# Complemented update gate, expert 0 inside the recurrence and 320 fixed places for each other expert

## The chip, the cores and the metric

One NeuronCore of a Trainium2 chip runs the whole program. The metric is the device time of one execution in microseconds (us), the median of a few runs. Engines are named as the profile names them: PE is TensorE (PEld its weight loads), DVE is VectorE, ACT is ScalarE, POOL is GpSimd, SP is SyncE, which here only issues DMAs.

## What is computed

Two transformer-like blocks over x (8 sequences, 256 steps, width 128; 2048 tokens). Only the recurrence and the first mixture of experts are touched:

```python
# _L0_cond2_ref: a GRU over the sequence (batch 8, 256 steps here)
r = sigmoid(xr_t + h @ W_hr)           # xr_t = x_t @ W_ir + b_ir
z = sigmoid(xz_t + h @ W_hz)
n = tanh(xn_t + r * (h @ W_hn + b_hn))
h_new = (1.0 - z) * n + z * h
# _L0_ffn_ref: top-1 routing; an expert keeps its 320 tokens of highest
# probability, the tokens dropped fall back to expert 0
final_e = where(keep, top1_idx, 0)
h = relu(tokens @ W1[e] + b1[e])       # 128 -> 512
y = h @ W2[e] + b2[e]                  # 512 -> 128, added where final_e == e
x = x + y
```

Before these stand an adaptive conditioning, a local attention and a linear attention; after them a second gated recurrence, a differential attention and a second, top-2, mixture of experts. All of it is float32; a float32 product is two passes of PE (the profile counts each).

## The kernel before

The program is a row of blocks; at the end of a block all engines wait for one another. In order: `setup`, `local_attention`, `linear_attention`, `gru_scan`, `route_top1`, `sparse_ffn`, `gate_scan`, `diff_attention`, `sparse_experts`. Every instruction order is written out by hand, with semaphores; no planner moves anything.

`gru_scan` (L782 to L956). x lies transposed, features on partitions, tokens in the order step by step, 8 tokens each. `hist` holds the states, two columns a token (the second is the state), 16 columns a step. G = 16 steps form a group; the input products of a group (`inputs`, L859) are written into PSUM ahead of time, 128 columns for each of r, z and n, and four bias rows are added by one-row products, seven products a group. In step s PE waits for the state and multiplies it by W_hr (8 columns, `pre_r`), W_hn and W_hz (`pre_n`, `pre_z`); the last two read 128 columns, the 8 states of now and 120 columns of places not yet written, whose contributions are zero (L881 to L889). Then come spare products of bf16 identities into `gspare`, three of 512 columns (`FILL`; two where an input product stands in the step). ACT: sigmoid of r (L921), sigmoid of z (L923), tanh of n (L925). DVE: a scan over 16 columns that forms xn + r * (...) (`narg`, L945), 1 - z (`keepz`, L949), z * h (`mix`, L950) and a scan that forms (1-z) * n + z * h (L953), which is the next state. Once a group the states are turned to token rows (PE L875, ACT L917) and stored in `hrow` by SP (L846). POOL clears `hist` at the start (L852), SP loads both expert weights and the biases b1 and b2 spread over the partitions (`b1B`, 2 MB). After the last step: one turn, then 16 router products (L904).

`route_top1` (L959) finds each token's expert, its probability and its rank within the expert, and `kept`. `sparse_ffn` (L1162): DVE counts the tokens of each expert, lays the experts out one after the other in blocks of 128 places (L1336 to L1369), and turns places into lists: `in_blk`, `in_lane`, a product into `f_inv` (L1380 to L1413), with the expert number of each block (L1391 to L1398). Then 23 blocks (`SLOTS`) are worked off: POOL gathers 128 rows of `hrow` (L1465), PE turns them (L1245), multiplies by W1 of the block's expert (L1254, 512 columns), DVE adds b1 (L1425), PE turns the hidden layer (L1263), ACT applies relu (L1318), PE multiplies by W2 (L1271), DVE adds b2 (L1431) and POOL scatters the rows into `frow` (L1474). POOL issues eight gathers first, then one gather and one scatter in turn. When all have landed SP reads `frow` back (L1483), PE turns it (L1294) and DVE adds it to x (L1442).

`gate_scan` (L1487) is the second recurrence, one product of 8 columns a step and 14 spare products of 128 columns.

## Time and profile before

| | us |
|---|---|
| median of 3 runs (lowest, highest) | 1709.58 (1707.33, 1715.83) |
| profiled execution | 1722.3 |
| its span, first to last instruction | 1720.3 |

| stage (from the timeline) | from, us | to, us |
|---|---|---|
| gru_scan, first step to last state | 571.6 | 1013.2 |
| its router products, to the end of the block | 1013.3 | 1021 |
| route_top1 | 1021 | 1058.7 |
| sparse_ffn, lists | 1058.7 | 1071.1 |
| sparse_ffn, 23 blocks and the way back | 1071.1 | 1155.5 |

The page gives PE 90% busy, DVE 46%, ACT 32%, POOL 8%. In a recurrence PE's busy time is mostly spare products, so the share says nothing of what bounds it; a timeline of one step does. A number after a line number is that of kernel.py.

### The profile page before, as it was taken

Reading aid. Unit: us, or ns where it says so; the run is one execution under the profiler, and the core shown is the slowest. Engines: PE = TensorE matmul, PEld = TensorE weight load, DVE = VectorE, ACT = ScalarE, POOL = GpSimd, SP = SyncE. Lnnn points to the kernel's source line nnn. Section 1 sums busy time; section 2 is a strip of 40 time slices with the busy share of each in tenths; the row PEclk is TensorE's granted clock in tenths of the full one; section 3 lists DMA queues with packets and bytes.
Section 4 is the critical chain, followed back from the end, with each engine's and each line's share of the span. In section 5 each row is a group of like instructions: output and inputs, shape, how many; then the busy total and the mean of one; then the engine's idle time right before and its main releaser. Section 6 shows DMA issues by size and latency. Waiting matters only on the chain. (4 is left out here: it accounts for less than half of the span.)

```text
span 1720.3 us, 28719 instructions
## 1 busy us (share of the span) xinstructions
PE 1541.4 (90%) x10500; PEld 1085.5 (63%) x10500; DVE 797.1 (46%) x2729; ACT 555.1 (32%) x2000; POOL 139.2 (8%) x189
## 2 busy tenths in 40 slices
PE   7999889879999899999999985879999999866995
PEld 5666556537777556566665652558888888744663
DVE  2777867655545333333333338333333333575223
ACT  2211221136554222222222220223444443533442
POOL 0000000000000000000000001630000000002662
PEclk9989998889999999999999985989999999977998
DMA  4000000000000400000000000120000000001113
GB/s 145 1 1 1 0 1 0 1 0 1 1 1 1 160 4 3 4 4 3 4 3 4 2 4 4 43 73 22 26 20 26 20 20 2 2 1 44 42 44 91
DMA packets 33892, 35.59 MB, mean 21 GB/s; under 512 B 3381, under 2 KB 27418, under 8 KB 33498
## 3 DMA queue, kind: packets, MB, share of 16 engines
q1 hardware_dynamic: 25674, 21.42, 4.1%
q0 software_dynamic: 3968, 8.13, 1.6%
q10 hardware_dynamic: 4112, 4.19, 0.8%
q8 instruction: 86, 1.41, 0.3%
q14 instruction: 52, 0.43, 0.1%
HBM read 26.53 MB, written 7.21 MB: 20 GB/s over the span
## 5 line engine op out<-in xcount | busy, mean ns | idle before, releaser
L1612 PE MATMUL spare<-identb 128*128 128x128 bf16 x3166 | 218.9, 220 | 0.0
L1612 PEld LDWEIGHTS spare<-identb 128*128 128x128 bf16 x3166 | 202.4, 103 | 4.3
L897 PE MATMUL gspare<-identb 128*128 128x512 bf16 x663 | 186.2, 381 | 0.0
L888 PEld LDWEIGHTS pre_r<-hist,gru_w 128*128 128x128 f32 x512 | 76.5, 188 | 139.0 <-DVE hist L953 138.0
L291 PE MATMUL sc<-headsel,prod 128*128 128x128 f32 x1024 | 163.3, 313 | 0.7 <-DVE prod L436 0.7
L291 PEld LDWEIGHTS sc<-headsel,prod 128*128 128x128 f32 x1024 | 141.4, 216 | 26.2 <-issue 23.9
L945 DVE TENSOR_TENSOR_SCAN narg<-rz,pre_n 128x16 f32<-128x16 f32 x256 | 48.0, 187 | 226.9 <-PE pre_n L888 226.9
L888 PE MATMUL pre_n<-hist,gru_w 128*128 128x128 f32 x512 | 121.5, 318 | 0.0
L888 PE MATMUL pre_r<-hist,gru_w 128*128 128x8 f32 x512 | 98.3, 264 | 23.9 <-DVE hist L953 2.9
L921 ACT ACTIVATE rz<-pre_r 128x8 f32<-128x8 f32 x256 | 45.7, 178 | 225.8 <-PE pre_r L888 225.8
L1663 DVE TENSOR_TENSOR_SCAN targ<-gates,pairs 128x16 f32<-128x16 f32 x256 | 49.1, 192 | 141.4 <-ACT gates L1622 141.4
L1582 PEld LDWEIGHTS s_pre<-s,wT 128*128 128x128 f32 x512 | 77.2, 190 | 40.7 <-ACT s L1625 40.0
L1582 PE MATMUL s_pre<-s,wT 128*128 128x8 f32 x512 | 98.1, 264 | 2.1 <-ACT s L1625 0.4
L888 PE MATMUL pre_z<-hist,gru_w 128*128 128x128 f32 x512 | 99.7, 275 | 0.0
L1660 DVE TENSOR_SCALAR pairs<-s,leak 128x8 f32<-128x8 f32 x256 | 59.6, 233 | 70.6 <-ACT s L1625 70.5
L1622 ACT ACTIVATE gates<-s_pre 128x8 f32<-128x8 f32 x256 | 45.6, 178 | 108.6 <-PE s_pre L1582 108.6
L1625 ACT ACTIVATE s<-targ 128x8 f32<-128x8 f32 x256 | 53.4, 209 | 83.9 <-DVE targ L1663 83.9
L485 DVE TENSOR_TENSOR term<-bc,kb 128x512 f32<-128x512 f32 x96 | 63.2, 685 | 33.2 <-PE bc L313 33.1
L888 PEld LDWEIGHTS pre_n<-hist,gru_w 128*128 128x128 f32 x512 | 78.0, 193 | 0.0
L897 PEld LDWEIGHTS gspare<-identb 128*128 128x128 bf16 x663 | 59.5, 97 | 28.8 <-issue 0.6
L888 PEld LDWEIGHTS pre_z<-hist,gru_w 128*128 128x128 f32 x512 | 77.4, 188 | 0.0
L923 ACT ACTIVATE rz<-pre_z 128x8 f32<-128x8 f32 x256 | 45.6, 178 | 97.3 <-PE pre_z L888 97.3
(413 smaller groups left out, 2531.2 us busy)
## 6 DMA issues: line engine op xcount, KB each, us to landing
w<-in_L_ffn_W SPq DMA_DIRECT2D x1, 2048.0 KB, 10.3
b1B<-in_L_ffn_b SPq DMA_DIRECT2D x1, 2048.0 KB, 19.9
raw<-in_L_ffn_wg SPq DMA_DIRECT2D x8, 256.0 KB, 3.3
raw<-in_L_ffn_wu SPq DMA_DIRECT2D x8, 256.0 KB, 2.7
raw<-in_L_ffn_wd SPq DMA_DIRECT2D x8, 256.0 KB, 2.6
wqkv<-in_L_attn_Wqkv SPq DMA_DIRECT2D x1, 1536.0 KB, 6.4
hrow<-htok SPq DMA_DIRECT2D x16, 64.0 KB, 1.5
f_back<-frow SPq DMA_DIRECT2D x4, 256.0 KB, 3.8
```

The source lines that it names most:

```text
L291: mm = nc.tensor.matmul(sc[:, :, :, :].rearrange("p i j h -> p (i j h)"), prod[u % 2][:, j, P * i:P * i + P], headsel[:, P - 2 * k:2 * P - ...
L485: nc.vector.tensor_tensor(term[s % 2][:, j, :], bc[g % 2][:, :], key(u, j, 512 * m, 512), ALU.mult).then_inc(term_done, 1)
L888: nc.tensor.matmul(out, n.gru_w[:, i, :], h, start=False, stop=True, skip_group_check=True).then_inc(ready, 1)
L897: nc.tensor.matmul(spare[:, :, :], n.identb[:, :], n.identb[:, :].unsqueeze(1).broadcast_to([P, 4, P]), start=True, stop=True)
L921: nc.scalar.activation(second(rz[s % 2][:, 0:16]), gate_slot(pre_r, s), ACT.Sigmoid).then_inc(r_done, 1)
L923: nc.scalar.activation(second(rz[s % 2][:, 16:32]), gate_slot(pre_z, s), ACT.Sigmoid).then_inc(z_done, 1)
L945: V.tensor_tensor_scan(narg[p][:, :], rz[p][:, 0:16], n_slot(s), 0.0, ALU.mult, ALU.add).then_inc(narg_done, 1)
L1582: nc.tensor.matmul(pre[s // G % 2][:, at:at + B], wT[:, 0, :], s2[:, 8 * s:8 * s + B], start=False, stop=True, skip_group_check=True).then ...
L1612: nc.tensor.matmul(spare[:, 0:P], n.identb[:, :], n.identb[:, :], start=True, stop=True)
L1625: nc.scalar.activation(s2[:, 8 * s + 8:8 * s + 16], second(targ[s % 2][:, :]), ACT.Tanh).then_inc(state, 1)
L1660: nc.vector.tensor_scalar(second(pair), s2[:, 8 * s:8 * s + 8], leak[:, 0:1], None, ALU.mult).then_inc(leaked, 1)
L1663: nc.vector.tensor_tensor_scan(targ[s % 2][:, :], gates[s % 2][:, :], pair, 0.0, ALU.mult, ALU.add).then_inc(arg_done, 1)
```

## The change

1. Recurrence. The three state products all have 8 columns. The biases of r, z and n leave PE (four of the seven products of a group stay) and become bias columns of the activations: b_ir of the sigmoid of r, and, with a scale of -1, minus b_iz and minus b_in of the two others. The sigmoid then gives 1 - z (`fresh`) and the tanh gives minus n. One DVE instruction forms (fresh - 1) * h, and the scan forms fresh * (-n) and subtracts, which is the new state; `keepz` is gone. The clearing of `hist` is gone.
2. Expert 0 is computed for all tokens inside the recurrence, a group behind: turn at step 1 of the group, four products by W1 at steps 2 and 3, four relus (ACT, with b1 as bias column) at steps 4 to 7, four products by W2 at steps 8 and 9, b2 added by DVE at step 10, and a store of 128 rows into `frow` (SP). Steps hold sixteen spare units (a unit is 128 columns of bf16), less what real products take: 14 in the turn's step, 8 in a step with expert products, 12 in one with an input product. The last group is done after the router products, before the block's end.
3. `route_top1` ends with each token's place, 384 * expert + rank, or one beyond all blocks if dropped (one instruction more in the chain, one beside it). `sparse_ffn` has no counts, offsets or owners. It works off experts 1 to 7, each with blocks of 128, 128 and 64 places: W1 is now the stationary operand, 4 products of 320 columns, relu with b1 as bias column on ACT, then 12 products by W2; 21 gathers and 21 scatters. `b1B` is not loaded.

```diff
-                    for out, i, ready, h in ((gate_slot(pre_r, s), 3, r_pre, h), (n_out, 5, n_pre, ahead), (z_out, 4, z_pre, ahead)):
+                    for out, i, ready in ((gate_slot(pre_r, s), 3, r_pre), (first(n_slot(s)), 5, n_pre), (gate_slot(pre_z, s), 4, z_pre)):
...
+                    units = 16
+                    if g >= 1 and k == TURN:
+                        turn(g - 1)
+                        units = 14
+                    elif g >= 1 and k in (HID, HID + 1):
+                        hidden(g - 1, 2 * (k - HID))
+                        hidden(g - 1, 2 * (k - HID) + 1)
+                        units = 8
+                    elif g >= 1 and k in (OUT, OUT + 1):
+                        output(g - 1, 2 * (k - OUT))
+                        output(g - 1, 2 * (k - OUT) + 1)
+                        units = 8
+                    elif g + 1 < GROUPS and 0 <= k - FEED < 4:
+                        inputs(g + 1, k - FEED)
+                        units = 12
+                    fill(units)
                 pe.wait_ge(state, T + 1)
-                turn(GROUPS - 1)
...
                 mm.then_inc(all_logits, 1)
+                turn(GROUPS - 1)
+                for f in range(NF):
+                    hidden(GROUPS - 1, f)
+                for f in range(NF):
+                    output(GROUPS - 1, f)
...
-                    nc.scalar.activation(second(rz[s % 2][:, 0:16]), gate_slot(pre_r, s), ACT.Sigmoid).then_inc(r_done, 1)
+                    nc.scalar.activation(second(reset[s % 2][:, :]), gate_slot(pre_r, s), ACT.Sigmoid, bias=bir).then_inc(r_done, 1)
...
-                    nc.scalar.activation(second(rz[s % 2][:, 16:32]), gate_slot(pre_z, s), ACT.Sigmoid).then_inc(z_done, 1)
+                    nc.scalar.activation(second(fresh[s % 2][:, :]), gate_slot(pre_z, s), ACT.Sigmoid,
+                                         bias=minus[:, 0:1], scale=-1.0).then_inc(z_done, 1)
...
-                    nc.scalar.activation(first(mix[s % 2][:, :]), second(narg[s % 2][:, :]), ACT.Tanh).then_inc(n_done, 1)
+                    nc.scalar.activation(first(mix[s % 2][:, :]), second(narg[s % 2][:, :]), ACT.Tanh,
+                                         bias=minus[:, 1:2], scale=-1.0).then_inc(n_done, 1)
...
-                    V.tensor_scalar(second(keepz[p][:, :]), z, -1.0, 1.0, ALU.mult, ALU.add).then_inc(z_used, 1)
-                    V.tensor_tensor(second(mix[p][:, :]), z, second(at_step(s)), ALU.mult).then_inc(z_used, 1)
+                    V.scalar_tensor_tensor(second(mix[p][:, :]), second(fresh[p][:, :]), 1.0, second(at_step(s)),
+                                           ALU.subtract, ALU.mult).then_inc(mixed, 1)
...
-                    V.tensor_tensor_scan(at_step(s + 1), keepz[p][:, :], mix[p][:, :], 0.0,
-                                         ALU.mult, ALU.add).then_inc(state, 1)
+                    V.tensor_tensor_scan(at_step(s + 1), fresh[p][:, :], mix[p][:, :], 0.0,
+                                         ALU.mult, ALU.subtract).then_inc(state, 1)
+                    if g >= 1 and k == OUT + 2:
+                        keep_output(g - 1)
...
+                def hidden(x):
+                    if x >= MINE:
                         return
+                    pe.wait_ge(x_kept, x + 1)
                     for f in range(NF):
+                        if x >= 1:
+                            pe.wait_ge(hid_done, NF * (x - 1) + f + 1)
+                        nc.tensor.matmul(h_ps[f][:, 0:CAPACITY], w1[:, x + 1, P * f:P * f + P], xT[x % 2][:, :],
+                                         start=True, stop=True).then_inc(h_in, 1)
...
                 turn_in(0)
                 turn_in(1)
                 hidden(0)
+                for x in range(MINE):
+                    hidden(x + 1)
+                    turn_in(x + 2)
+                    down(x)
...
                 pool.wait_ge(lists, 1)
+                for x in range(4):
+                    gather(x)
+                for x in range(MINE):
+                    scatter(x)
+                    if x + 4 < MINE:
+                        gather(x + 4)
```

## Rows read from the trace of the kernel before

**Rows 1.** windows of TensorE's clock: us, busy (x) by engine, PEclk, DMA share, GB/s
```profile
1090.00:1146.00 56.00, 46.32 (x282) 33.95 (x280) 18.29 (x38) 14.74 (x35) 32.22 (x33) 1.00 0.13 40
```

**Rows 2.** timeline of one step: start, duration, engine, line [idle before <-releaser]
```profile
713.86 0.30 PEld L888 LDWEIGHTS pre_r<-hist,gru_w 128*128 128x128 f32 x2 [0.61 <-DVE hist L953]
...
714.29 0.18 ACT L921 ACTIVATE rz<-pre_r 128x8 f32<-128x8 f32 x1 [0.88 <-PE pre_r L888]
714.31 0.30 PEld L888 LDWEIGHTS pre_z<-hist,gru_w 128*128 128x128 f32 x2
...
714.65 0.81 PE L897 MATMUL gspare<-identb 128*128 128x512 bf16 x3
714.69 0.19 DVE L945 TENSOR_TENSOR_SCAN narg<-rz,pre_n 128x16 f32<-128x16 f32 x1 [0.88 <-PE pre_n L888]
714.85 0.18 ACT L923 ACTIVATE rz<-pre_z 128x8 f32<-128x8 f32 x1 [0.38 <-PE pre_z L888]
714.92 0.20 ACT L925 ACTIVATE mix<-narg 128x8 f32<-128x8 f32 x1
715.06 0.17 DVE L949 TENSOR_SCALAR keepz<-rz 128x8 f32<-128x8 f32 x1 [0.18 <-ACT rz L923]
715.14 0.16 DVE L950 TENSOR_TENSOR mix<-rz,hist 128x8 f32<-128x8 f32 x1
715.33 0.19 DVE L953 TENSOR_TENSOR_SCAN hist<-keepz,mix 128x16 f32<-128x16 f32 x1
715.58 0.30 PEld L888 LDWEIGHTS pre_r<-hist,gru_w 128*128 128x128 f32 x2 [0.61 <-DVE hist L953]
```

**Rows 3.** groups by shape, ScalarE with a bias column: xcount | busy, mean ns
```profile
L369 ACT ACTIVATE kb<-pj,cols 128x512 f32<-128x512 f32 x32 | 22.0, 687 | 16.8 <-PE pj L279 16.8
...
L369 ACT ACTIVATE kb<-pj,cols 128x8 f32<-128x8 f32 x16 | 4.2, 261 | 0.0
```

**Rows 4.** timeline, two such activations back to back in local attention
```profile
27.22 0.85 ACT L369 ACTIVATE kb<-pj,cols 128x512 f32<-128x512 f32 x2 [0.17 <-PE pj L279]
```

**Rows 5.** timeline, spare products and next weights early in the second recurrence
```profile
1160.91 1.65 PE L1612 MATMUL spare<-identb 128*128 128x128 bf16 x14
...
1162.25 0.55 PEld L1582 LDWEIGHTS s_pre<-s,wT 128*128 128x128 f32 x2
```

**Rows 6.** timeline, start of the recurrence
```profile
569.10 2.45 DVE L939 COPY hist<-cols 128x8 f32<-128x8 f32 x1
```

**Rows 7.** windows after the last step: clock while the router products run
```profile
1017.00:1020.50 3.50, 3.48 (x17) 3.39 (x16) 0.00 (x0) 0.00 (x0) 0.00 (x0) 0.50 0.00 0
```

**Rows 8.** the page, DMA issues: KB each, us to landing
```profile
hrow<-htok SPq DMA_DIRECT2D x16, 64.0 KB, 1.5
```

**Rows 9.** timeline, from the routing to the lists of places
```profile
1058.72 0.20 DVE L1336 TENSOR_SCALAR f_dropped<-r_kept 128x16 f32<-128x16 f32 x1 [0.70 <-PEq L1077]
...
1060.32 0.15 POOL L1458 IOTA f_dump<- 128x24 f32 x1
...
1065.44 0.56 DVE L1380 TENSOR_TENSOR f_in_blk<-f_blk_ramp,f_hi_f 128x384 bf16<-128x384 f32 x1
...
1070.93 0.18 DVE L1413 TENSOR_SCALAR f_src_i<-f_dst_i 128x24 int32<-128x24 int32 x1
```

**Rows 10.** timeline, start of the expert loop
```profile
1071.42 1.21 POOL L1465 DMA_INDIRECT f_xg<-hrow,f_src_i  x1 [10.94 <-DVE f_src_i L1413]
...
1074.57 0.45 PE L1245 MATMUL f_x_ps<-ident,f_xg 128*128 128x128 f32 x1 [5.15 <-DMA f_xg<-hrow,f_src_i]
...
1076.46 3.78 PE L1254 MATMUL f_h_ps<-w,f_xgT 128*128 x4 [0.49 <-ACT f_xgT L1309]
```

**Rows 11.** groups of GpSimd: xcount | busy us, mean ns | idle before
```profile
L1474 POOL DMA_INDIRECT frow<-f_y,f_dst_i x23 | 22.7, 985 | 22.9 <-DVE f_y L1431 19.8 <-issue 3.0
L1465 POOL DMA_INDIRECT f_xg<-hrow,f_src_i x23 | 22.4, 973 | 17.6 <-DVE f_src_i L1413 10.9 <-issue 6.7
```

**Rows 12.** timeline, end of the expert loop
```profile
1145.05 0.97 POOL L1474 DMA_INDIRECT frow<-f_y,f_dst_i  x1 [0.83 <-DVE f_y L1431]
```

More of the change, by code:

```diff
@@ L779, in _, with gru_scan @@
                     add(b)
-def gru_scan(nc, n, a, hist, hrow, w1, w2, b1B, b2B, logits):
+def gru_scan(nc, n, a, hist, hrow, frow, w1, w2, b2B, logits):
     G = P // B
@@ L877, in _, with hidden, output @@
-                for i in range(7):
+                        pe.wait_ge(y_kept, g)
+                    nc.tensor.transpose(turn_ps, tokens(g), n.ident[:, :]).then_inc(h_turned, 1)
+                def hidden(g, f):
+                    if g == 0 and f == 0:
+                        pe.wait_ge(n.load_experts, 48)
+                    pe.wait_ge(h_kept, g + 1)
+                    nc.tensor.matmul(h_ps[:, f, :], w1[:, 0, P * f:P * f + P], tokens(g), start=True, stop=True).then_inc(hid_in, 1)
+                def output(g, f):
+                    pe.wait_ge(hid_done, NF * (g + 1))
+                    nc.tensor.matmul(y_ps, hid[:, f, :], w2[:, 0, f, :], start=(f == 0), stop=(f == NF - 1)).then_inc(y_in, 1)
@@ L878, in _, with fill @@
+                def fill(units):
+                    for _ in range(units // 4):
+                        nc.tensor.matmul(spare[:, :, :], n.identb[:, :], n.identb[:, :].unsqueeze(1).broadcast_to([P, 4, P]),
+                                         start=True, stop=True)
+                    for _ in range(units % 4):
+                        nc.tensor.matmul(spare[:, 0, :], n.identb[:, :], n.identb[:, :], start=True, stop=True)
+                for i in range(4):
                     inputs(0, i)
@@ L1368, in _ @@
[L1368 to L1371 removed]
+                done(V.tensor_copy(pos_i[:, :], place[:, :]))
                 after()
@@ new lines, in scatter @@
+                def scatter(x):
+                    for k in range(BLKS):
+                        c, r = BLKS * (x + 1) + k, rows(k)
+                        pool.wait_ge(y_kept, 2 * x + 1 + (k == BLKS - 1))
+                        pool.indirect_dma_start(out=frow[:, :],
+                                                out_offset=bass.IndirectOffsetOnAxis(ap=dst_i[0:r, c:c + 1], axis=0),
+                                                in_=ysb[0:r, x, k, :], in_offset=None).then_inc(scattered, 16)
```

397 lines of the change are left out of this document (143 added, 254 removed).

## The prediction

> **What bounds the kernel now.** I read the page first, then a timeline of a few steps of the first recurrence, then the timeline from its end to the second recurrence, then ScalarE's groups by shape. The page's busy shares don't help here, because most of PE's products in a recurrence are spare ones; what counts is the order in which one step's results arrive. In the step of [rows 2] time zero is the load of the weights of r at 713.86. ACT begins the sigmoid of r at +0.43, DVE `narg` at +0.83, ACT the sigmoid of z at +0.99, the tanh at +1.06, DVE `keepz` at +1.20, `mix` at +1.28, the state's scan at +1.47, and the next step's load stands at +1.72. The tanh ends at +1.26, but the scan waits until `mix` has ended at +1.44: the path through z is late, not the one through n. The three spare products end at +1.60, 0.12 before the next load; PE is not the bound, but not far from it. The step takes 1.715 us, 256 of them 439 us. After the recurrence the lists take 12 us [rows 9], and the expert loop 74.9 us from 1071.1, the end of the lists, to 1146.0 [rows 9, 12]. POOL is busy there for 45.1 us with 46 indirect DMAs and has about 0.30 us of issue beside each; 19.8 us it waits for y [rows 11].
>
> **Part by part. 1, the step.** Products of 8 columns: the loads of r and z stand 0.45 apart, so one product's pair of loads costs 0.22. From its own load to its reader r (8 columns) takes 0.43 and z (128 columns) 0.54 [rows 2]; with 8 columns z takes 0.43 too and its sigmoid begins at 0.44 + 0.43 = +0.87, 0.12 earlier. n is then ready at 0.22 + 0.43 = +0.65. Bias columns: the same 8-column activation takes 0.178 without a bias column and 0.261 with one [rows 3]; so 0.083 for each of three, and the tanh, 0.20 now, comes to 0.285 [rows 2, 3]. The new step: sigmoid of r +0.43 to +0.69; `narg` 0.10 later, +0.79 to +0.98 (ACT to DVE is 0.03; `narg` stood behind n before, so I take 0.10, the upper side); the sigmoid of z +0.87 to +1.13. Tanh: `narg` allows it 0.23 after its own start, at +1.02; ACT itself lets a biased activation begin 0.10 before the one ahead ends (one of 0.687 and one of 0.261 take 0.85 together [rows 3, 4]), at +1.03. Tanh to +1.32, scan possible at +1.35. Through z: +1.13, `mix` in its new form +1.16 to +1.32 (0.16, as the old one), scan possible at +1.35. Both paths now come in together. Scan +1.35, next load 0.25 later: 1.60. Of the 0.24 that the shorter z and the missing `keepz` give, the two biased activations in the way take back about half. Saved: 0.115 x 256 = **29.4 us**. Were bias columns free, the scan would stand at +1.27 and the step at 1.51; were ACT to run the three strictly one after another, tanh +1.13 to +1.42, the step would be 1.70. These are the two ends, 52 and 4 us saved; I take 1.60, since a row of the very shape exists.
>
> **2, what shares the step.** PE: six weight loads 0.65, spares from about +0.75; four of 0.22 each end streaming at +1.61, and the first product of the next step, whose load stands at +1.60, needs them gone by +1.71. They fit, with 0.1 to spare, as long as weights may be loaded while a spare streams. The expert's products replace spares at their own price (two float32 passes of 0.11 for four units). On ACT a relu of 128 x 128 with bias stands behind the tanh, about 0.36 us from +1.2 to +1.6; the next sigmoid is at +2.03: hidden, and what is queued behind it waits for nothing. DVE adds b2 (0.3) behind the scan at +1.54; the next `narg` is at +2.4: hidden. SP's second store a group waits for y and holds up only the next `hrow` store, 8 steps later. If this cover were gone, 64 relus would cost up to 23 us. No cost.
>
> **3, start and end.** The first copy into `hist` took 2.45 us beside POOL's clearing and ended at 571.55 [rows 6]. Without it four products of about 0.22 stand between 569.1 and the first step, 570.0: **-1.6**. After the last state the router products are the same, but now the last group of expert 0 hangs behind them, at half clock, the level 0.50 that [rows 7] shows from 1017: turn and copy 0.75, hidden 4 x 0.43 + 0.2, relus 1.2, output 4 x 0.43 + 0.2, add 0.4, store and its landing 1.9 (1.5 in [rows 8]) and SP's turn. That is 8.1, of which 0.5 (the logits' copy and the turn of before) was there already: **+7.6** (6 to 9).
>
> **4, lists.** `route_top1` gets one more link of 0.2 and a neighbour: **+0.3**. The work from 1058.72 to the conversion of places goes; `in_blk` then stands 0.9 behind the block's start: four short DVE links need 0.8, POOL's constants, which ended at 1060.47 before, end 0.9 after its start since two clears and a count row ahead of them are gone [rows 9]. So 1059.6 instead of 1065.44, -5.8, and the owner's chain ahead of the last conversion gives 0.3: **-6.1**.
>
> **5, the expert loop.** T0 is the end of the lists. POOL has 42 DMAs of 1.25 to 1.29 (0.97 or 0.99 and 0.30): 53.8 with the long first one [rows 10, 11]. I find no row of 64 partitions; between full price and half of the busy part the fourteen short ones give up to 6 us; I take full price. PE: 12 gathers go first; those of the first expert have landed at T0 + 6.0 (one landed 1.94 after its issue ended [rows 10]), those of the second at 9.7, and PE turns both before its first hidden product. That one runs at half clock: 3.78 us for four passes of 512 columns [rows 10], so 8 passes of 320 columns 4.3. Then the second expert's hidden 2.1, and 12 products by W2, 24 passes of 0.11, 2.6: first y at T0 + 20.9, while POOL was done gathering at 15.6. POOL stands 5.4 us. Afterwards expert and gather take turns: gathers 5 to 7 are queued behind scatters 1 to 3, and each expert's output behind the turn of the one two further on. Laid out step by step, y of the experts comes at 26, 34, 41.5, 49, 54 and 56.5, POOL stands another 2.1, and the last scatter is issued at T0 + 61.5. Against 74.9: **-13.4** (range 57 to 65 us). Relu of 128x320 with bias is about 0.53, as long as one of the four products: covered.
>
> Sum: -29.4 - 1.6 + 7.6 + 0.3 - 6.1 - 13.4 = -42.6 us. The profiled execution took 1722.3, so 1679.7 for such a one; the median of the runs is 12.7 lower, and the change should be the same there: 1709.6 - 42.6 = **1667 us**. Two DMAs more in `setup` stand beside the load of x, and two loads fewer elsewhere: nothing.
>
> A page rule on step 2: the Trainium skill, "TensorE: Matmul & The Clock Gate", Part 3, says that LDWEIGHTS overlaps a running MATMUL only when the row groups differ; here they are the same. By it PE would be the bound, and that is the second rival below. The trace speaks against it: in [rows 5] the weights of a float32 product are being loaded at 1162.25, 0.3 us before the spare products end at 1162.56.
>
> **The rivals.** A, the sum above: 1667, own range 1655 to 1678.
> B, the expert loop loses the full clock. PE is busy two thirds of that loop and stands 2 to 2.5 us before each late turn; before it was busy 46.3 of 56 us with a clock of 1.00 [rows 1]. If it falls to half once the gaps begin, the last scatter comes at T0 + 71 to 76, 9 to 14 later, with a fall from the start 23 later: 1677 to 1690.
> C, PE becomes the bound of the step: if the next weights wait until the last spare has drained, four spares (0.81 for three, 1.03 for four) end at 0.75 + 1.03 = +1.78 and the step is 1.80, 1.85 in the eight steps of a group with expert or input products. It decides from 1.715 on. 256 x 0.115 = 29.4 more than before instead of less: 1709.6 + 29.4 - 13.2 = 1726, slower than before. For it: the end of the spares at +1.60 is only 0.12 ahead of the load. Against it: [rows 5].
> D, bias columns cost nothing once the semaphore has come: step 1.51, 1644. Against it the lengths of [rows 3].
> E, relu under the sigmoid table needs a table load and one back: a load after each relu group would give over 100 us. Copy and tanh run under it without one in this trace; relu under it is not shown.
> The Trainium skill, "ScalarE: Activation LUTs", Table sets, says that relu is in every set; no row here shows it beside sigmoid. By it E falls away.
>
> **How the numbers follow.** A 0.60, B 0.18, C 0.08, D 0.08, E 0.02, and 0.04 for a size of mine that is off by enough to end near 1709. The measurement of this kernel tells about 0.5% (8.5 us) from no change. Faster: A, B and D, 0.86. Same: 0.05. Slower: C (most of it) and E, 0.09. The range reaches from D's 1644, which is also the end of free bias columns, to 1692, B's worst with a step of 1.61; it leaves out C, E and the remainder, 0.14.
>
> **What would show it.** Right: a step of 1.60 with sigmoid rows of 0.26 and a tanh of 0.285; the sigmoid of z 0.87 behind the load; the state's scan waiting for tanh and `mix` by turns; PE waiting for the state about 0.1 us a step; 8 us from the end of the router products to the block's end; POOL idle about 5 us before its first scatter. Wrong: activations still 0.18; PE's weight load of r no longer waiting for DVE; a clock below 1.00 within the expert loop; a table load inside the recurrence. The sum is most at the mercy of the step: 0.01 us there is 2.6 us in the end.

## The result, and the profile after

The changed kernel took 1700.7 us in the median of six runs, the kernel before 1712.1 beside it: a ratio of 0.993, 95% interval 0.990 to 0.995. In a second comparison it was 1705.0 against 1721.2, 0.991 (0.988 to 0.994). So it is faster, by 11 to 16 us, which is less than 1%; the forecast was 42.6 us, a time of 1667 with a range that ended at 1692.

In some executions TensorE's clock fell to half at the beginning of the recurrence and stayed there to its end; these took 2005 to 2022 us (one of the six, the one that was profiled first, took 2011), and ratios are of the others. Here are the two kinds on the page, the first of a later run of the same kernel at full clock, the second of the first profile (each slice is a fortieth of the span):

```profile
span 1699.3 us, 28619 instructions
PEclk9988899889999999999999975879999999977998
```

```profile
span 2009.5 us, 28619 instructions
PEclk9988899799965555555555555556799999995998
```

All readings of stages below are of the first, at 1701.0 us with its surroundings, against the profiled execution of before.

| stage, us | before | after | difference | forecast |
|---|---|---|---|---|
| first step to last state | 441.6 | 431.9 | -9.7 | -29.4 |
| last state to the block of routing | 7.9 | 15.7 | +7.8 | +7.6 |
| routing | 37.6 | 37.5 | -0.1 | +0.3 |
| lists | 12.4 | 6.5 | -5.9 | -6.1 |
| end of lists to the last scatter | 74.9 | 67.5 | -7.4 | -13.4 |
| from there to the end | 574.3 | 574.3 | 0.0 | 0 |
| sum | | | -15.3 | -41.0 |

The forecast had 1.6 us more for an earlier first step. The time of the first step doesn't show it: it stands at 571.61 before and at 565.95 after, and between 565.95 and 573.42 in seven profiles of kernels that start like the changed one, since the stages ahead of the recurrence scatter by that much. Counted from the table load of ScalarE with which the block starts (568.23 before, 564.18 after) it is 3.38 us before and 1.77 after: the 1.6 are there. The difference of the two profiles, 21.0 us, is the 15.3 of the table, these 1.6 and 4.1 of scatter ahead of the block; the second comparison gives 15 to 16.

**A step**, timeline (time, duration, engine, line; in brackets what it waited for), the rows that answer to [rows 2]:

```profile
620.25 0.30 PEld L898 LDWEIGHTS pre_r<-hist,gru_w 128*128 128x128 f32 x2 [0.46 <-DVE hist L997]
...
620.67 0.27 ACT L951 ACTIVATE reset<-pre_r,cols 128x8 f32<-128x8 f32 x1 [0.78 <-PE pre_r L898]
...
620.94 1.02 PE L886 MATMUL gspare<-identb 128*128 128x512 bf16 x4
620.97 0.19 DVE L990 TENSOR_TENSOR_SCAN narg<-reset,pre_n 128x16 f32<-128x16 f32 x1 [0.78 <-ACT reset L951]
621.12 0.27 ACT L953 ACTIVATE fresh<-pre_z,g_minus 128x8 f32<-128x8 f32 x1 [0.18 <-PE pre_z L898]
621.29 0.29 ACT L956 ACTIVATE mix<-narg,g_minus 128x8 f32<-128x8 f32 x1
621.42 0.17 DVE L993 SCALAR_TENSOR_TENSOR mix<-fresh,hist 128x8 f32<-128x8 f32 x1 [0.26 <-ACT fresh L953]
621.68 0.19 DVE L997 TENSOR_TENSOR_SCAN hist<-fresh,mix 128x16 f32<-128x16 f32 x1
621.92 0.30 PEld L898 LDWEIGHTS pre_r<-hist,gru_w 128*128 128x128 f32 x2 [0.46 <-DVE hist L997]
```

The step is 1.67 (1.675 in most, 1.687 in the mean of 255). Behind the first load: sigmoid of r +0.42, `narg` +0.72, sigmoid of z +0.87, tanh +1.04 to +1.33, `mix` +1.17 to +1.34, scan +1.43. Everything up to the tanh's end is within 0.07 of the forecast, most within 0.01; the scan was forecast at +1.35.

**The end of the recurrence** ([rows 7, 8] of before end in one copy and one turn):

```profile
1005.03 0.29 DVE L1002 COPY logits<-pre_r 128x128 f32<-128x128 f32 x1 [7.20 <-PE pre_r L920]
...
1005.67 2.07 PE L878 MATMUL gh_ps<-hist,w 128*128 128x128 f32 x8 [0.37 <-ACT htok L939]
1007.78 1.14 ACT L945 ACTIVATE ghid<-gh_ps,cols 128x128 f32<-128x128 f32 x4 [2.16 <-PE gh_ps L878]
...
1008.97 2.08 PE L882 MATMUL gh_ps<-w2e,ghid 128*128 128x128 f32 x8 [1.23 <-ACT ghid L945]
1011.09 0.29 DVE L983 TENSOR_TENSOR ytok<-gh_ps,b2B 128x128 f32<-128x128 f32 x1 [5.76 <-PE gh_ps L882]
...
1013.49 0.20 POOL L1050 MEMSET before<- 128x128 f32 x1 [997.23 <-POOLq L836]
```

Link by link what the forecast listed: hidden 2.07, relus 1.14, output 2.08, add 0.29, then 2.1 from the store's issue to the next block.

**Lists and expert loop** ([rows 9 to 12]): timeline of two links; then the groups of GpSimd in the loop (xcount | busy us, mean ns | idle before), and windows with TensorE's clock (the last three numbers are granted clock, DMA share, GB/s):

```profile
1051.02 0.18 DVE L1346 CAST f_pos_i<-r_place 128x16 int32<-128x16 f32 x1 [0.30 <-PEq L1124]
...
1052.20 0.56 DVE L1356 TENSOR_TENSOR f_in_blk<-f_blk_ramp,f_hi_f 128x384 bf16<-128x384 f32 x1 [0.43 <-POOL f_dump L1410]
```

```profile
L1422 POOL DMA_INDIRECT frow<-f_y,f_dst_i x21 | 20.1, 958 | 20.9 <-DVE f_y L1397 15.7 <-issue 5.2
L1415 POOL DMA_INDIRECT f_xg<-hrow,f_src_i x21 | 20.0, 954 | 11.8 <-issue 6.1 <-DVE f_src_i L1379 5.7
```

```profile
1063.00:1073.00 10.00, 5.63 (x13) 3.46 (x14) 0.98 (x2) 1.18 (x3) 7.45 (x8) 0.50 0.20 48
1073.00:1083.00 10.00, 10.00 (x56) 7.62 (x55) 1.60 (x4) 5.14 (x10) 2.32 (x3) 0.98 0.04 13
...
1097.00:1101.00 4.00, 4.00 (x20) 3.71 (x21) 1.01 (x3) 1.78 (x4) 2.55 (x3) 0.57 0.11 37
```

GpSimd is busy for 40.1 us and issues for 11.3, 51.4 in all (forecast 53.8; the short DMAs take 0.91), but waits 15.7 us for y where 7.5 were forecast. TensorE's clock is half until 16 us into the loop (to about 1073.5) and again in two stretches of 3.4 us (in the windows 1097 to 1101 and 1107 to 1111).

### The profile page after: what moved, and what is told of

The parts are those of the page before. It is cut to its first block and busy times, and to the rows that moved or that the text cites. A ratio compares the mean times of both kernels' runs of the same rounds, so it can differ in the third digit from the quotient of the medians.

```text
span 2009.5 us, 28619 instructions
## 1 busy us (share of the span) xinstructions
PE 1854.6 (92%) x10754; PEld 1360.7 (68%) x10754; DVE 759.1 (38%) x2445; ACT 637.1 (32%) x2046; POOL 129.9 (6%) x179
## 3 DMA queue, kind: packets, MB, share of 16 engines
q8 instruction: 87, 1.43, 0.3%
## 5 line engine op out<-in xcount | busy, mean ns | idle before, releaser
L886 PE MATMUL gspare<-identb 128*128 128x512 bf16 x829 | 400.1, 626 | 0.0
L898 PEld LDWEIGHTS pre_r<-hist,gru_w 128*128 128x128 f32 x512 | 170.0, 336 | 88.2 <-DVE hist L997 34.0
L990 DVE TENSOR_TENSOR_SCAN narg<-reset,pre_n 128x16 f32<-128x16 f32 x256 | 47.8, 187 | 457.3 <-PE pre_n L898 455.0
L951 ACT ACTIVATE reset<-pre_r,cols 128x8 f32<-128x8 f32 x256 | 68.7, 268 | 390.5 <-PE pre_r L898 390.5
L886 PEld LDWEIGHTS gspare<-identb 128*128 128x128 bf16 x829 | 124.4, 163 | 98.1 <-issue 90.2
L898 PE MATMUL pre_z<-hist,gru_w 128*128 128x8 f32 x512 | 146.8, 361 | 0.0
L898 PE MATMUL pre_n<-hist,gru_w 128*128 128x8 f32 x512 | 146.8, 361 | 0.0
L898 PEld LDWEIGHTS pre_n<-hist,gru_w 128*128 128x128 f32 x512 | 139.6, 332 | 0.0
L898 PEld LDWEIGHTS pre_z<-hist,gru_w 128*128 128x128 f32 x512 | 139.6, 332 | 0.0
L953 ACT ACTIVATE fresh<-pre_z,g_minus 128x8 f32<-128x8 f32 x256 | 68.7, 268 | 149.3 <-PE pre_z L898 149.1
```

The source lines that it names most:

```text
L886: nc.tensor.matmul(spare[:, :, :], n.identb[:, :], n.identb[:, :].unsqueeze(1).broadcast_to([P, 4, P]), start=True, stop=True)
L898: nc.tensor.matmul(out, n.gru_w[:, i, :], h, start=False, stop=True, skip_group_check=True).then_inc(ready, 1)
L951: nc.scalar.activation(second(reset[s % 2][:, :]), gate_slot(pre_r, s), ACT.Sigmoid, bias=bir).then_inc(r_done, 1)
L953: nc.scalar.activation(second(fresh[s % 2][:, :]), gate_slot(pre_z, s), ACT.Sigmoid, bias=minus[:, 0:1], scale=-1.0).then_inc(z_done, 1)
L990: V.tensor_tensor_scan(narg[p][:, :], reset[p][:, :], n_slot(s), 0.0, ALU.mult, ALU.add).then_inc(narg_done, 1)
```

## Where the step's gain went

Theory STEP: a link of the step is longer than forecast, at full clock. Theory CLOCK: in part of the recurrence the clock is at half. To measure a step in executions that are not profiled, both kernels were cut to 128 of 256 steps; the other half of the states is a copy, so they compute something else, but do the rest of the work as it was:

```diff
-                for s in range(T):
+                for s in range(T // 2):
...
+                V.tensor_copy(hist[:, 16 * (T // 2 + 1):16 * (T + 1)], hist[:, 16:16 * (T // 2 + 1)]).then_inc(state, T // 2)
```

> The changed kernel's first recurrence runs only 128 of its 256 steps; one copy on VectorE fills the other half of the states with the first (about 2 us), and the stores of the second half repeat the first half's buffers. So the outputs are those of another input from step 128 on, and the time against the full kernel is 128 steps less the copy. It gives the length of a step in executions that are not profiled. If a step takes 1.60 there: 1700.7 - 205 + 3 = 1499. If it takes 1.71 to 1.72: 1484. If the clock falls at some moment in the recurrence, the result lies outside these two.

> The same cut in the kernel before: 128 of 256 steps, a copy of about 2 us in their place. A step of 1.715, as in the profiled execution, gives 1711 - 219.5 + 3 = 1494.5. A step that is shorter in executions that are not profiled (the profiled execution took 12.7 us more than their median) gives up to 12 us more than that.

1490.9 us and 1507.4, where the full kernels took 1705.0 and 1723.3. The copy takes 1.23. A step of the changed kernel is (1705.0 - 1490.9 + 1.2) / 128 = 1.68, one of before 1.70. This is rough: the 1705.0 was measured later, beside a kernel before of 1721.2 instead of 1723.3, and the first step's scatter of up to 8 us between profiles is 0.06 a step. The traces are sharper. In the full kernel's profile the clock is 1.00 from the first step to the last and the steps take 1.675; the cut kernels' own profiles have 216.0 us for 128 steps after and 221.4 before, 1.69 and 1.73 in the mean; and the profiled execution (1701.0) took no longer than the three beside it (1704 to 1706). So STEP holds: the lost 20 us are there in every step, at full clock.

Which step of the chain? First the biases, then TensorE's own load, were changed. All three biases back on TensorE:

```diff
-                    nc.scalar.activation(second(reset[s % 2][:, :]), gate_slot(pre_r, s), ACT.Sigmoid, bias=bir).then_inc(r_done, 1)
+                    nc.scalar.activation(second(reset[s % 2][:, :]), gate_slot(pre_r, s), ACT.Sigmoid).then_inc(r_done, 1)
```

(and the same for the two others, with seven products a group again).

> The changed kernel with the three input biases back on TensorE as one-row products (seven products a group, in steps 11 to 14, spares reduced to 8 units there), so that sigmoid and tanh run without a bias column. Everything computed stays the same. The bias theory expects activations of 0.178, 0.178 and 0.20 us instead of 0.26, 0.26 and 0.285, and at full clock a step of 1.51 to 1.54 us instead of 1.60: about 20 us less over 256 steps. If TensorE is the bound at full clock, the activations get shorter and the step stays within 0.03 us of that of the changed kernel. CLOCK expects a stretch at half clock at the start here too.

In this kernel the product of b_in replaces x's part of n in group 0 instead of being added. The next one adds it.

> The biases of r, z and n are again added by three products a group on the tensor engine, before the steps, and the three activations have no bias column; everything else is the changed kernel's. Theory ACT (the step is set by the chain over ScalarE and VectorE, as the prediction's sum has it): each of the two biased activations on the chain gives back 0.08 and the step gets 0.07 shorter, 18 us for 256 steps, so about 1682. Theory PE (the tensor engine's own work of three products and four spares sets the step): nothing changes on the chain that counts, 1700 within 3.

Both ran at full clock only for the first 19 and 49 us of the recurrence (2018.6 and 1996.6 us in all, the next section). In those stretches the step was 1.53 to 1.54 (in steps without input products): with the bias columns gone the chain gets 0.14 shorter while TensorE does the same. From the second run:

```profile
572.95 0.30 PEld L900 LDWEIGHTS pre_r<-hist,gru_w 128*128 128x128 f32 x2 [0.42 <-DVE hist L1002]
...
573.64 1.02 PE L888 MATMUL gspare<-identb 128*128 128x512 bf16 x4
...
574.48 0.30 PEld L900 LDWEIGHTS pre_r<-hist,gru_w 128*128 128x128 f32 x2 [0.31 <-DVE hist L1002]
```

The four spares end at 574.66, and the next weights are loaded from 574.48. The chain over ScalarE sets the step, not TensorE.

> One of the four spare products of 512 columns is left out of every step (and one of the fewer ones in the steps with other products). Theory PE: the step gets shorter by up to 0.12, 1672 to 1685. Theory ACT: the step stays, 1700 within 3, as long as the clock stays at its upper level. Theory CLOCK (the missing time is a stretch of the recurrence at half clock, because the tensor engine has too little to do): less work makes that stretch longer, 1710 to 1950.

1898 us, at half clock from 594 on. At full clock, before that, its step is 1.68 as with the fourth spare (the load of r stands at 588.84 and at 590.52). Theory PE, the prediction's rival C, is out.

Last the tanh alone, with b_in on TensorE and the two sigmoids as in the changed kernel:

```diff
-                    nc.scalar.activation(first(mix[s % 2][:, :]), second(narg[s % 2][:, :]), ACT.Tanh,
-                                         bias=minus[:, 1:2], scale=-1.0).then_inc(n_done, 1)
+                    nc.scalar.activation(first(mix[s % 2][:, :]), second(narg[s % 2][:, :]), ACT.Tanh,
+                                         scale=-1.0).then_inc(n_done, 1)
```

> Of the three biases only b_in is added by a product again (one more a group, in a step that gives up one spare), so the tanh has no bias column and takes 0.20 instead of 0.29; the two sigmoids keep theirs. In the changed kernel the tanh ends 1.33 behind the first weights, mix 1.34, and the scan starts 1.43. Theory TANH (the scan follows the end of the tanh by 0.10 and mix by 0.03): the tanh now ends at +1.24, the scan starts behind mix at +1.37, the step goes from 1.675 to 1.62, 14 us: 0.8% below the changed kernel. Theory MIX (this form of mix is what the scan waits for, 0.09 behind it): the scan stays at +1.43 and the time at 1.675 a step.

Its clock fell too (2004 us), at 595, but of its first fourteen steps, at full clock, thirteen take 1.62. Timeline of one:

```profile
575.43 0.20 ACT L957 ACTIVATE mix<-narg 128x8 f32<-128x8 f32 x1
575.57 0.17 DVE L994 SCALAR_TENSOR_TENSOR mix<-fresh,hist 128x8 f32<-128x8 f32 x1 [0.26 <-ACT fresh L954]
575.77 0.19 DVE L998 TENSOR_TENSOR_SCAN hist<-fresh,mix 128x16 f32<-128x16 f32 x1
576.01 0.30 PEld L899 LDWEIGHTS pre_r<-hist,gru_w 128*128 128x128 f32 x2 [0.40 <-DVE hist L998]
```

`mix` is the same instruction at the same place, ends at 575.74, and the scan follows it by 0.03. The load before stands at 574.39 (0.43 ahead of the sigmoid of r at 574.82), so the step is 1.62. Theory TANH holds: the scan comes 0.10 behind a tanh, 0.03 behind a `mix`. The run with only n wide (next section) shows the same without any bias: there tanh and `mix` end together and the scan comes 0.10 later.

```profile
601.13 0.21 ACT L969 ACTIVATE mix<-narg 128x8 f32<-128x8 f32 x1
601.17 0.17 DVE L1007 SCALAR_TENSOR_TENSOR mix<-fresh,hist 128x8 f32<-128x8 f32 x1
...
601.44 0.19 DVE L1011 TENSOR_TENSOR_SCAN hist<-fresh,mix 128x16 f32<-128x16 f32 x1
```

In the kernel before the tanh was done 0.18 ahead of `mix`, so this link was not to be seen there.

What makes this link 0.10 stands in the second recurrence of the same trace. Its DVE instruction `pairs` follows a tanh of the same size. It waits for that tanh alone, except in steps 64, 128 and 192, where it first waits for a semaphore of TensorE and then for the tanh's (timeline of the changed kernel, steps 63 and 64):

```profile
1218.40 0.21 ACT L1580 ACTIVATE s<-targ 128x8 f32<-128x8 f32 x1 [0.33 <-DVE targ L1618]
1218.64 0.23 DVE L1615 TENSOR_SCALAR pairs<-s,leak 128x8 f32<-128x8 f32 x1 [0.28 <-ACT s L1580]
...
1219.59 0.21 ACT L1580 ACTIVATE s<-targ 128x8 f32<-128x8 f32 x1 [0.33 <-DVE targ L1618]
...
1219.90 0.23 DVE L1615 TENSOR_SCALAR pairs<-s,leak 128x8 f32<-128x8 f32 x1 [0.35 <-ACT s L1580]
```

It starts 0.03 to 0.04 behind the tanh in 252 steps and 0.10 behind it in those three, in this profile and in that of before (0.10 to 0.11). `targ`, which waits for DVE's own `pairs` and then for a sigmoid, starts 0.09 to 0.11 behind that sigmoid in 254 of 256 steps. In the first recurrence `mix` waits for the sigmoid of z alone and `narg` for the sigmoid of r first and TensorE's n second: 0.02 to 0.04 in 256 and 254 steps. The scan waits for `mix` first and for the tanh second: 0.10 to 0.11 in 252. So it is not the tanh: 0.07 are added where the semaphore that comes last is the second that DVE waits for. No run exchanged the two waits of the scan.

## When the clock stays down

> The changed kernel once more, unaltered, for a trace of an undisturbed execution. The one trace at hand had TensorE at half clock through the whole recurrence, with a step of 2.80 us. Theory CLOCK: an undisturbed execution of 1700 us also begins the recurrence at half clock and stays there for some 25 to 30 steps of 2.8 us (33 us over the forecast divided by 1.2 us a step), and its steps at full clock take 1.60 us. Theory STEP: the clock is at 1.00 from the first few steps on, as in the kernel before, and every step takes about 1.72 us, because TensorE or the path through z ends it.

2022.2 us, half clock from 573.6 to the end of the recurrence.

> The changed kernel once more, on the chip of the runs beside it. Theory RANDOM (where the clock falls at the start of the recurrence or in a step with fewer spare products, it stays down; whether it falls differs from execution to execution): some executions near 1700 and some near 2010, and nothing much between. Theory PROFILE (only the profiled execution falls): the timed ones stay at 1695 to 1712, the profiled one at 2010.

Four executions, 1701.0 to 1706.0; the profiled one is the one read above. So it is not the profiler: the same kernel does both, and two variants of it in the last section, whose recurrence is the same, did both within one comparison (1700 and 2005). RANDOM holds. What happens is in the windows, first of before, then of the changed kernel's first profile:

```profile
568.00:572.00 4.00, 2.38 (x17) 2.10 (x18) 3.16 (x8) 1.28 (x1) 3.30 (x1) 1.00 0.53 142
572.00:576.00 4.00, 4.00 (x16) 2.51 (x17) 1.24 (x8) 0.91 (x6) 0.00 (x0) 0.57 1.02 383
576.00:580.00 4.00, 3.76 (x24) 2.49 (x24) 1.24 (x8) 1.07 (x7) 0.00 (x0) 1.00 1.06 304
```

```profile
568.00:572.00 4.00, 2.64 (x17) 2.07 (x18) 1.29 (x10) 2.04 (x4) 0.00 (x0) 0.97 0.38 86
572.00:576.00 4.00, 4.00 (x16) 2.65 (x14) 0.74 (x4) 0.95 (x5) 0.00 (x0) 0.50 1.02 380
...
600.00:1000.00 400.00, 400.00 (x1493) 297.17 (x1492) 76.44 (x419) 109.28 (x452) 0.00 (x0) 0.50 0.01 3
```

In both the clock falls behind a gap of TensorE, which is busy for 2.4 and 2.6 of the 4 us from 568 to 572. Before, it is back in the next window; in the changed kernel it never comes back, though TensorE is busy without a gap: its work now sets the step, about 2.8 us, the four spares alone taking 1.87. The page's busy share, 100% there, doesn't tell that it would rise.

> Eight spare products of 512 columns are issued ahead of the recurrence, where the tensor engine stood 1.5 us before the input products of group 0. Everything else is the changed kernel's. If the clock is lost to that gap alone, it stays at 1.00 from 570 on in every execution, and the times are 1695 to 1712. If the steps with expert or input products lose it by themselves, it falls within the first groups as it does without the burst, 1990 to 2030. The burst itself costs under 0.5 us.

```diff
+                fill(32)
                 pe.wait_ge(n.load_later, n.later_loads)
```

(The two waits of TensorE that stood ahead of the input products come behind the burst.) 1705.8 us, ratio 0.991, and no execution of five stayed down. Five of five is no proof: the kernel without the burst had four of four beside it, with a gap of the same 1.5 us and a clock of 1.00 in its profile, and of 20 executions with this whole recurrence and no burst five stayed down. The profiles of all kernels together say more: without a burst the clock fell at the start of the recurrence in seven of fifteen, with it in none of three (two of them in the last section). But the gap is not the only place: with the biases on TensorE it fell at 587 and 621, with three spares at 594, with the plain tanh at 595, each time within or just behind a group's steps with input products. All of these have fewer spares there than the changed kernel, and in no profile of the changed kernel did it fall there.

> The products of n and z have 128 columns again, with three spare products a step, as in the kernel before, with the zeroed states that they need; the biases are added by products. What is left of the change is the complemented gate, expert 0 inside the recurrence and the places. The sigmoid of z then starts 0.98 after the first weights and takes 0.18, mix +1.19 to +1.36, the state's scan +1.39, the next step +1.63: 0.085 less than before, 22 us. With 13 us of the other parts: 35 us below the kernel before. If the wide products are what keeps the clock at its upper level, it stays at 1.00 through the recurrence as it does in the kernel before; if not, 1990 to 2030.

```diff
-                    for out, i, ready in ((gate_slot(pre_r, s), 3, r_pre), (first(n_slot(s)), 5, n_pre), (gate_slot(pre_z, s), 4, z_pre)):
+                    for out, i, ready, h in ((gate_slot(pre_r, s), 3, r_pre, h), (n_out, 5, n_pre, ahead), (z_out, 4, z_pre, ahead)):
...
-                    fill(units)
+                    fill(units - 4)
```

> The whole step of the kernel before (z itself, keepz, wide products, three spares, biases by products) with expert 0 inside the recurrence and the 320 places. The step stays at 1.715; what is left is the sum of the other parts, 13 us below the kernel before, and if the clock holds, the difference to the run with wide products and the complemented gate is that gate alone, 22 us. If the clock falls here too, the expert's products inside the steps are what loses it, since nothing else of the tensor engine's work in a step differs from the kernel before.

1695.7 us, ratio 0.986 (0.982 to 0.989), and 1714.2, ratio 0.996 (0.994 to 0.998). The windows of the first, and the ones of the narrow products with the biases on TensorE:

```profile
572.00:576.00 4.00, 4.00 (x19) 2.75 (x18) 1.06 (x6) 0.71 (x5) 0.00 (x0) 0.69 1.05 370
576.00:580.00 4.00, 3.85 (x22) 2.07 (x20) 1.49 (x9) 1.18 (x8) 0.00 (x0) 1.00 1.05 292
```

```profile
620.00:624.00 4.00, 4.00 (x19) 2.99 (x18) 0.73 (x4) 0.66 (x5) 0.00 (x0) 0.59 0.00 0
...
628.00:1280.00 652.00, 652.00 (x2414) 483.96 (x2413) 121.89 (x668) 117.39 (x724) 0.00 (x0) 0.50 0.01 3
```

With wide products the clock fell at the start and was back four microseconds later, as before; with expert 0 inside the steps it held for the rest of the recurrence. The gate alone is worth 18.5 us of the 22 expected (steps of 1.65 and 1.73 in the mean). Of the other parts the run with the old gates shows 7 us instead of 13: the terms of the table, +7.8 - 0.1 - 5.9 - 7.4, give 5.6.

> The run with wide products, but only n has 128 columns; z has eight again; three spares, biases by products, zeroed states. The sigmoid of z starts at about +0.88 and takes 0.18, mix +1.09 to +1.26; narg stays at +0.83 (n is wide), the tanh +1.06 to +1.26, the scan behind it at +1.36, the step 1.60: 0.04 less than with both wide (1.64), 10 us. If one wide product is enough to bring the clock back after a fall, the clock is 1.00 through the recurrence; if it takes both, it falls in the first groups and stays down, 1850 to 1950.

1695.8 us, ratio 0.982 (0.978 to 0.986). The clock fell four times in its profile, at 572, 671, 859 and 913, for 41 us in all, and came back each time (the mean is 0.95 over the recurrence). So one product of 128 columns in a step was enough to bring it back, and with both it also held. That is what these runs show. Why the spares, bf16 products of an identity with 512 columns, don't do the same wasn't settled: no run changed their type, their data or their width alone. The sum of columns doesn't explain it: by the program the narrow kernel moves 2096 a step, the one with both wide 2064, and the one with n wide, which also came back, 1824.

## The end of the recurrence and the expert loop

> The changed kernel with the last group of expert 0 spread between the sixteen router products: the turn ahead of them, the hidden products after three of them, the output products after nine, and VectorE adds b2 ahead of the copy of the logits. If the 7.8 us between the copy of the logits and the next block are that chain and nothing else, about 4 go: the products' own time (about 3.9 at half clock) stays, their waits for ScalarE, the add, the store and its landing are hidden. If they are the block's end or the stores' landing, under 1 us goes.

```diff
                 pe.wait_ge(state, T + 1)
+                turn(GROUPS - 1)
                 for k in range(NBLK):
+                    if k == 3:
+                        for f in range(NF):
+                            hidden(GROUPS - 1, f)
+                    if k == 9:
+                        for f in range(NF):
+                            output(GROUPS - 1, f)
```

```profile
1001.36 1.16 PE L878 MATMUL gh_ps<-hist,w 128*128 128x128 f32 x8
...
1002.55 1.14 ACT L947 ACTIVATE ghid<-gh_ps,cols 128x128 f32<-128x128 f32 x4 [1.92 <-PE gh_ps L878]
1004.87 2.06 PE L882 MATMUL gh_ps<-w2e,ghid 128*128 128x128 f32 x8
...
1010.33 0.21 POOL L1052 MEMSET before<- 128x128 f32 x1 [994.12 <-POOLq L836]
```

From the last state (999.88) to the next block it is 10.45 us instead of 15.66: 5.2 off, where 4 were expected for the waits, the add and the store that the router products now cover. The hidden products, which now come while the clock is still high (1.16 instead of 2.07), give 0.9 of the rest. The median is 1699.4, ratio 0.985 (0.980 to 0.990), in which the scatter of the start also lies; one of the four executions was of the kind whose recurrence stays at half clock (2005). So most of the 7.8 us was order, not work.

> The changed kernel with 34 spare products in the expert loop, where the tensor engine waits for the first two experts' rows (24 ahead of the first turn, 10 ahead of the second). In the changed kernel's fast profile the clock stood at half for the first 27 us of the loop and in two dips of 3.4 us, and the last scatter ended 67.2 behind the first gather, against 61.5 in the profile where the clock rose earlier. Theory B (the half clock is what the loop lost against the forecast): the clock is at 1.00 from the first hidden product on, the last scatter ends 56 to 62 behind the first gather, 5 to 9 us less in the whole. Theory POOL (GpSimd's own 42 DMAs and their places set the length): 65 to 67, no change.

```diff
+                warm(24)
                 turn_in(0)
+                warm(10)
                 turn_in(1)
```

Windows and GpSimd's scatters in the profile at full clock in the recurrence:

```profile
1058.00:1061.00 3.00, 3.00 (x8) 1.03 (x7) 0.70 (x5) 0.00 (x0) 1.60 (x2) 0.50 0.02 5
1061.00:1102.00 41.00, 35.02 (x188) 24.01 (x186) 5.22 (x14) 12.01 (x24) 26.44 (x29) 1.00 0.14 38
1102.00:1109.00 7.00, 4.83 (x21) 4.16 (x22) 0.49 (x1) 0.00 (x0) 3.69 (x4) 0.51 0.13 37
```

```profile
L1429 POOL DMA_INDIRECT frow<-f_y,f_dst_i x21 | 20.2, 960 | 17.5 <-DVE f_y L1404 12.4 <-issue 5.2
```

From the first gather to the last scatter it is 63.9 instead of 67.2, and the wait for y 12.4 instead of 15.7: 3.3 us, less than the 5 expected. The changed kernel's first profile has no dips in the loop, and there the clock rose 10.6 us into it: 61.5, and 9.7 us of waiting. GpSimd's single waits for y in the three (7.4, 2.9, 3.7 and 1.7 us in the changed kernel; 3.5, 3.1, 4.0 and 1.7 with the spares; 6.0, none, 2.0 and 1.7 without dips) tell more than their sums. The spares took 3.9 off the first wait, the one that a late rise of the clock lengthens. The third, in which the last dip lies, is 1.7 to 2.0 longer than without one. But the second, 2.9 and 3.1, lies ahead of any dip in the one and at full clock in the other. It is a stand of DVE:

```profile
1089.40 3.07 PE L1300 MATMUL f_y_ps<-w2e,f_hid 128*128 128x128 f32 x24
...
1097.14 0.42 DVE L1395 TENSOR_TENSOR f_y<-f_y_ps,b2B 128x256 f32<-128x256 f32 x1 [6.67 <-remote]
```

The products of this y end at 1092.47, and DVE adds b2 to them 4.7 us later, in the profile without dips at once (0.04). ScalarE stands at the same time, until 1097.20. With the spares it is the same at 1094.79. The profile names no engine for it, and no run looked for the cause. So theory B holds for a part only: by these waits, of the 5.7 us between 67.2 and 61.5 about 3 are the clock's and 2.9 are this stand. (Two of the four executions were of the kind whose recurrence stays at half clock, so the time alone says nothing here.)

## What beats both

> The run with wide n and z and the complemented gate, put together with the spread last group of expert 0, the 34 spare products in the expert loop, and eight spare products ahead of the recurrence. The step stays at 1.64 to 1.65. The run with wide products alone stood 25 below the kernel before (ratio 0.9855); the spread group took 5.2 off between the last state and the next block, the spares 3.3 off the expert loop, the spares at the start 1 to 2. Sum: 35 below the kernel before, a ratio of 0.980, and no execution in which the clock stays down.

1688.7 us against 1723.4, a ratio of 0.9785 (0.976 to 0.981), 35 us as forecast, in five executions from 1685.1 to 1690.7.

> The same with only n wide, and two more narrow spare products (14 units of 128 columns instead of 12) in every step. The step is 1.605 at full clock, as in the run with n wide, since the spares then end at +1.60 and the next product needs them gone at +1.70. In that run the clock fell three times in the recurrence, for 38 us in all, and came back. If two more units hold it, the recurrence gets 10 us shorter than with both wide and the ratio is 0.974; if it falls as often as before, the two are equal within 3 us; if it falls and stays down, 1900.

1690.2 us, 0.980 (0.978 to 0.983). In the profile its clock held from 372 to 997, but the four steps of a group with input products took 1.80, 1.79, 1.80 and 1.69, the three long ones with two input products beside the spares; the gain of the other twelve is gone into these four (422.2 us from first step to last state, with both wide 422.0). One of its six executions took 1712 with a mean clock of 0.918 instead of 0.932 to 0.937, so it may not always hold. The version with both wide is the better one.

## Why the prediction was wrong, step by step

- **Step 1, the step, -29.4: measured -9.7.** The chain was right up to its last link: sigmoids 0.27, tanh 0.29 (forecast 0.261 and 0.285 from [rows 3]), ScalarE letting the tanh start 0.10 before the sigmoid of z ends [rows 4], z 0.12 earlier. The failed sentence is "Tanh to +1.32, scan possible at +1.35": it took the 0.03 from ACT to DVE that [rows 2] show behind the sigmoid of z and put it behind the tanh, where it is 0.10, since there DVE waits for `mix` first and for the tanh second. With 0.01 of a longer tanh that is 0.075 a step, 19 us. [Rows 2] could not have shown it, as before the scan waited for `mix`; but the second recurrence of the same trace has 0.10 for a wait of this form in nearly every step, and 0.10 was at hand (the prediction took it for the sigmoid of r to `narg`, where 0.03 came out).
- **Rival D, free bias columns**, is out by the lengths. But the neighbourhood of its price was real: with no bias columns the step is 1.53 (forecast 1.51).
- **Rival C, TensorE the bound**, is out: in the step above the spares end at 621.96 and the next weights load from 621.92, three spares give the same step, and without bias columns the weights come 0.18 ahead of the spares' end and the step is 1.53. Its own sum has a slip: 1.80 and 1.85 in equal parts are 0.110 a step above 1.715, not 0.115. The rule of the Trainium skill, "TensorE: Matmul & The Clock Gate", Part 3, that LDWEIGHTS overlaps a running product only with other row groups, would have given 1.80; the trace disagrees with it at 1.67.
- **The earlier start, -1.6**, came out from the block's start: 3.38 to 1.77.
- **Step 2, what shares the step**, was right at full clock: the relus and the add cost nothing that shows (1.687 in the mean against 1.675; before 1.725 against 1.713). The spares end at +1.71 and not at +1.61; the 0.1 to spare wasn't there, and wasn't needed.
- **The clock in the recurrence** was taken as 1.00 with no sentence on it. The row was there: in before it falls at 572 and comes back. Spares were counted by their time, four for three and two wide products, and not asked whether they do for the clock what the real products did. This is the failure that matters most to a user, since it makes some executions 17% slower than before; no rival held it.
- **Step 3, end, +7.6: +7.8**, right in every link. It was forecast as given, and two thirds of it were order (5.2 us).
- **Step 4, lists, -6.1: -5.9**, and the route's +0.3 came out at -0.1.
- **Step 5, loop, -13.4: -7.4.** Rival B in part: it was forecast 9 to 14 us beyond the 61.5, and came to 6. The sum has the clock at full level from the end of the first hidden product on, about 16 us into the loop, and there it rose; but then it fell twice for 3.4 us. What failed is the full clock of the sum after that, for 3 of the 6, and that y is added as soon as its products end, for the other 3 (the stand of DVE, whose cause stays open). GpSimd's own 42 DMAs were 2.4 us shorter than forecast, its waits 8.2 longer. That the profile without dips has the sum's 61.5 is part luck: its waits are 2.2 longer than forecast (9.7 against 7.5), and the shorter DMAs pay for it.
- **Rival E** is out: no table load stands in the trace between the one at 564.18 and the one at 1013.49, with relu, sigmoid, tanh and copy between them. The Trainium skill, "ScalarE: Activation LUTs", Table sets, says that relu is in every set, and the trace agrees.

Sum: between the two profiles 26 us are missing against the table's forecast of 41; 20 of them are the step, nearly all one link, and 6 the loop, half clock and half a stand of DVE. The medians miss 31 in the first comparison and 26 in the second; the 5 between them are not explained.

## What to carry to other kernels

When a change makes another path the last one, the link at which the new path joins is new too: its latency is in no row of that loop before and needs a bound of its own, from a wait of the same form elsewhere in the trace, and in a loop of 256 steps 0.07 us are 18 us. Look at which of an instruction's waits ends last, the first or the second. Spare products that keep a clock up are to be compared with what they replace by whether the clock comes back after a fall, not by their time; look for a fall and its recovery in the windows of before. Work that is hung behind the last product of a block can often be put between products that are there anyway.

## What the runs showed of the hardware

- The granted clock takes two courses in one and the same kernel. In eleven profiles with narrow state products it stayed at 1.00 through the recurrence in five, and in six it fell and stayed down to the recurrence's end, for 599 to 742 us, with TensorE busy all the time. In the seven with a wide n, or n and z (the kernel before and its half among them), it fell up to four times, eight falls in all, and came back each time, or didn't fall (two, both with the burst).
- DVE starts 0.03 us behind the end of a ScalarE instruction if its semaphore is the only one or the first that DVE waits for (621.39 to 621.42, 1218.61 to 1218.64), and 0.10 behind it if it is the second (621.58 to 621.68, 1219.80 to 1219.90), with tanh and sigmoid alike.
- An indirect DMA over 64 partitions costs GpSimd 0.91 us and one over 128 about 0.97: half the rows save 6%.
